# Last stage of a four-layer attention network: the wide probabilities' squares go from partition to partition in 16 DMAs a batch instead of through DRAM

## The reference

```python
h = _layernorm(x, gamma, beta)
Q = (h @ Wq).reshape(B, NQ, N_HEADS, HEAD_DIM)
K = (context @ Wk).reshape(B, NC, N_HEADS, HEAD_DIM)
V = (context @ Wv).reshape(B, NC, N_HEADS, HEAD_DIM)
attn = jnp.einsum('bihd,bjhd->bhij', Q, K)
attn = jax.nn.softmax(attn, axis=-1) * scale
vals = jnp.einsum('bhij,bjhd->bihd', attn, V).reshape(B, NQ, INNER)
out = vals @ Wo + bo
return x + out
```

## Time and profile before

| | |
|---|---|
| median of 3 runs | 1729.83 us (1729.8 to 1731.36) |
| the profiled execution's own time | 1727.86 us |
| span of that execution, first to last instruction | 1726.1 us |
| PE busy | 1638.1 us (95%) |
| DVE, ACT, POOL busy | 1310.8, 1240.9, 677.3 us |
| bytes moved by DMA | 216.51 MB |

### The profile page before, as it was taken

How to read it: one execution, slowest core, us unless ns; L and a number is a source line. 1 busy time by engine, 2 the same in 40 slices (tenths; PEclk the granted TensorE clock), 3 DMA queues, 4 the chain that set the end, 5 groups by cost and what they waited for, 6 DMA issues and landing times. The chain is left out here.

```text
span 1726.1 us, 48944 instructions
## 1 busy us (share of the span) xinstructions
PE 1638.1 (95%) x16520; PEld 1351.9 (78%) x16520; DVE 1310.8 (76%) x2408; ACT 1240.9 (72%) x3858; POOL 677.3 (39%) x946
## 2 busy tenths in 40 slices
PE   7999999999999999989899998988999999999997
PEld 6888888888888888779777777867787888787875
DVE  5777777777777777747688887656888888888885
ACT  5777777777777777623388886456888888888885
POOL 3444444454444444413222222643343434343431
PEclk9999999999999999989999999999999999999999
DMA  7776777777767767730000000014434344343441
GB/s 198 198 189 185 190 194 187 219 208 205 194 184 190 186 188 185 209 86 1 1 2 0 0 0 1 0 38 135 137 118 134 118 127 124 121 131 119 133 131 53
DMA packets 230743, 216.51 MB, mean 125 GB/s; under 512 B 19874, under 2 KB 228324, under 8 KB 230628
## 3 DMA queue, kind: packets, MB, share of 16 engines
q1 hardware_dynamic: 230628, 215.17, 45.2%
HBM read 112.34 MB, written 102.76 MB: 125 GB/s over the span
## 5 line engine op out<-in xcount | busy, mean ns | idle before, releaser
L658 ACT ACTIVATE L_probs<-L_scores,L_neg_max 128x128 f32<-128x128 f32 x512 | 182.7, 386 | 134.6 <-DVE L_neg_max L740 134.6
L854 POOL TENSOR_TENSOR L_probs<-L_probs,L_inv_sum 128x1024 f32<-128x1024 f32 x128 | 242.8, 1897 | 88.4 <-DVE L_inv_sum L760 88.4
L734 DVE TENSOR_REDUCE L_row_max<-L_scores 128x8 f32<-128x1024 f32 x128 | 156.1, 1219 | 41.5 <-PE L_scores L534 41.5
L1957 POOL TENSOR_TENSOR L2L_w_probs<-L2L_w_probs,L2L_w_inv_sum 128x1024 f32<-128x1024 f32 x64 | 121.4, 1897 | 129.7 <-DVE L2L_w_inv_sum L1783 129.5
L766 DVE STREAM_TRANSPOSE L_squares<-L_probs 128x1024 f32<-128x1024 f32 x128 | 156.6, 1223 | 0.3 <-POOL L_probs L854 0.3
L581 PE MATMUL L_ring<-L_probsT,L_v 128*64 128x128 f32 x2048 | 127.9, 277 | 9.5 <-issue 8.6
L581 PEld LDWEIGHTS L_ring<-L_probsT,L_v 128*64 128x64 f32 x2048 | 111.2, 137 | 29.9 <-issue 27.0
L534 PE MATMUL L_scores<-L_kT,L_qT 64*128 64x128 f32 x2048 | 131.8, 278 | 0.9 <-ACT L_kT L647 0.9
L534 PEld LDWEIGHTS L_scores<-L_kT,L_qT 64*128 64x128 f32 x2048 | 119.4, 188 | 12.5 <-ACT L_oT L647 8.1
L750 DVE TENSOR_REDUCE L_sums<-L_probs 128x8 f32<-128x1024 f32 x64 | 78.1, 1220 | 66.1 <-ACT L_probs L665 66.1
L1581 ACT ACTIVATE L2L_w_probs<-L2L_scores,L2L_w_neg_max 128x128 f32<-128x128 f32 x256 | 90.5, 372 | 39.3 <-DVE L2L_w_neg_max L1747 39.3
(11 more groups left out here) (220 smaller groups left out, 4617.0 us busy)
## 6 DMA issues: line engine op xcount, KB each, us to landing
L_relay<-L_squares SPq DMA_DIRECT2D x128, 512.0 KB, 3.4
L_probsT<-L_relay SPq DMA_DIRECT2D x512, 128.0 KB, 3.6
L2L_relay<-L2L_w_squares SPq DMA_DIRECT2D x64, 512.0 KB, 3.4
L2L_w_probsT<-L2L_relay SPq DMA_DIRECT2D x256, 128.0 KB, 2.9
out_x<-x SPq DMA_DIRECT2D x32, 64.0 KB, 2.7
L0a_wq<-in_L_xattn_Wq SPq DMA_DIRECT2D x2, 256.0 KB, 3.1
L0a_wk<-in_L_xattn_Wk SPq DMA_DIRECT2D x2, 256.0 KB, 3.7
L0a_wv<-in_L_xattn_Wv SPq DMA_DIRECT2D x1, 512.0 KB, 6.5
```

Of the source, the lines that this page charges most:

```text
L658: done = nc.scalar.activation(slot_probs(at, 0)[:, n, :], scores[:, 0, r, i, :], ACT.Exp, scale=layer_of(at).scale, bias=neg_max[:, n:n + ...
L734: nc.vector.tensor_reduce(row_max[:, s, :], slot(s), AX.X, ALU.max).then_inc(max_ready[s], 1)
L854: nc.gpsimd.tensor_tensor(to, to, inv_sum[:, :, s, :].unsqueeze(3) .to_broadcast([TOKENS, 2, GROUP, TOKENS]), ALU.mult).then_inc(divided, 1)
L1957: nc.gpsimd.tensor_tensor(to, to, w_inv_sum[:, :, s, :].unsqueeze(3) .to_broadcast([TOKENS, 2, GROUP, TOKENS]), ALU.mult).then_inc(w_divid ...
```

## The change

The relay in DRAM and its semaphores are gone. `w_squares` gets a second buffer. SP's `carry(at)` waits until both halves of batch `at` are turned, and issues 16 DMAs, one for each pair of blocks (i, j), each of 32 partitions x 512 elements (all 16 heads, 64 KB), from `w_squares` straight to `w_probsT`. One semaphore for each buffer counts all 16, so both halves of `w_weigh` wait for all of them, and DVE's turn waits for the landing of the batch two before in place of the relay of the batch before.

```diff
-    LANDED = 16 * SQUARES
+    LANDED = 16 * SQUARES * SQUARES
-        w_squares = sb("w_squares", [TOKENS, SQUARES, HEADS, SQUARE])
+        w_squares = sb("w_squares", [TOKENS, 2, SQUARES, HEADS, SQUARE])
-        w_relayed = [sem("w_relayed_0"), sem("w_relayed_1")]
-        w_probsT_landed = [[sem(f"w_probsT_landed_{p}{h}") for h in range(2)] for p in range(2)]
-        w_relay = [nc.dram_tensor(f"{W.name}{N.name}_relay_{h}", [TOKENS, SQUARES, SLOT_HEADS, SQUARE], FP32).ap()
-                   for h in range(2)]
+        w_probsT_landed = [sem(f"w_probsT_landed_{p}") for p in range(2)]
...
-                w_landed(pe, at, s)
+                w_landed(pe, at)
...
-                if at.n >= 1:
-                    dve.wait_ge(w_relayed[s], at.times(16, 0))
-                nc.vector.transpose(w_squares[:, :, SLOT_HEADS * s:SLOT_HEADS * (s + 1), :]
+                if at.n >= 2:
+                    w_landed(dve, at.plus(-2))
+                nc.vector.transpose(w_squares[:, at.n % 2, :, SLOT_HEADS * s:SLOT_HEADS * (s + 1), :]
...
-            def away(at, h):
-
-                sp.wait_ge(w_squares_turned, at.times(2, h + 1))
-                if at.n >= 1:
-                    w_landed(sp, at.plus(-1), h)
-                sp.dma_start(w_relay[h], w_squares[:, :, SLOT_HEADS * h:SLOT_HEADS * (h + 1), :]
-                             ).then_inc(w_relayed[h], 16)
-
-            def back(at, h):
+            def carry(at):

                 p = at.n % 2
-                sp.wait_ge(w_relayed[h], at.times(16, 16))
+                sp.wait_ge(w_squares_turned, at.times(2, 2))
                 if at.n >= 2:
-                    await_filled(sp, f"w.PV{h}", at.plus(-2))
+                    await_filled(sp, "w.PV1", at.plus(-2))
                 for j in range(SQUARES):
-                    sp.dma_start(w_probsT[SQUARE * j:SQUARE * (j + 1), p, :, SLOT_HEADS * h:SLOT_HEADS * (h + 1), :],
-                                 w_relay[h].rearrange("(i b) j h a -> j b i h a", b=SQUARE)[j]
-                                 ).then_inc(w_probsT_landed[p][h], 16)
+                    for i in range(SQUARES):
+                        sp.dma_start(w_probsT[SQUARE * j:SQUARE * (j + 1), p, i, :, :],
+                                     w_squares[SQUARE * i:SQUARE * (i + 1), p, j, :, :]
+                                     ).then_inc(w_probsT_landed[p], 16)
...
                 if here(At(t), 0):
-                    away(At(t), 1)
-                    back(At(t), 1)
-                if here(At(t), 1):
-                    away(At(t + 1), 0)
-                    back(At(t + 1), 0)
+                    carry(At(t))
```

More of the change, by code:

```diff
@@ L1339, in n_slot, with w_landed @@
             return n_probs[:, at.n % 2, s, :, :]
-        def w_landed(engine, at, h):
-            engine.wait_ge(w_probsT_landed[at.n % 2][h], at.times(LANDED // 2, LANDED - LANDED // 2 * (at.n % 2)))
+        def w_landed(engine, at):
+            engine.wait_ge(w_probsT_landed[at.n % 2], at.times(LANDED // 2, LANDED - LANDED // 2 * (at.n % 2)))
         @block.tensor
```

## The result

The changed kernel takes 1811.57 us in the median of 4 runs (1810.06 to 1818.62), beside 1729.82 us for 4 runs of the kernel before: a ratio of 1.0479, with a 95% interval from 1.045 to 1.0509. It is 82 us slower, and far outside the predicted range. The profiled execution took 1810.06 us.

The account below looks back on a forecast made before the run. PE, busy for 95% of the span, was taken as the bound, the relay as hidden. Terms 2.3 + 1.0 + 1.9 + 0.3 = +5.5 us on the profiled 1727.86 gave 1733.4, or 1735.0 for the median; range 1730 to 1750.

Parts of the forecast that it names:

- The price of an issue: On SP, 15 steps between the 16 issues, mostly 0.475 us each: 7.0 us, bounds 6.5 and 8.7.
- The landing: Time from the last of the 16 issues to its arrival in `w_probsT`: 2.4 us, bounds 2.2 and 3.1.
- the sum had 9.5: Path from the end of DVE's turn to PE's weighing: 0.03 + 7.0 + 2.4 + 0.1 us, between 8.8 and 11.9.
- So d settles at e / 2: Steady steps: if the path exceeds its cover by e, PE's late start d comes to half of e.
- ACT's slack of 0.7 us: Steady steps: the halving holds until ACT's second copy runs out of 0.7 us; from there d = e - 0.7.
- The cover of 9.78: Steady steps: 9.78 us from a batch's last turn on DVE to PE's weighing of it, leaving 0.3 us to spare.
- The ends: Pipeline filling and draining: PE waits longer before weighing batches 0 (+2.3 us), 2 (+1.0) and 30 (+1.9); batch 31: 0.
- +0.3: Row of 16 issues on SP: allowance in us for single issues that take 1.52 us instead of 0.43.
- The terms of zero: Removed relay transfers, DVE's wait for a landing two batches before, SP's wait and store issues: each worth 0.
- The overrun in every step: Rival for the steady steps: pieces cost by number, 0.57 us each, path 11.4, time 1765 (1745 if milder); chance 0.22.
- The faster case: Rival: steps where the loop turns lose their extra 1 us, up to 6 turns, giving 1727 or 1724; chance 0.06.
- the 2.2 us to spare: Kernel before: the relay's last DMA lands at 1390.5, this long before PE begins weighing at 1392.69.

Follow-up runs that it names:

- experiment 3: Changed kernel with each of the 16 DMAs carrying 4 of 16 heads (16 KB) from batch 2 on: 1803.78 us, beside 1734.32 for the kernel before.
- experiment 4: Changed kernel with its 16 DMAs reading a weight matrix in DRAM instead of the squares in SBUF: 1746.04 us, beside 1734.32 for the kernel before.
- experiment 5: Changed kernel with 16 SBUF-to-SBUF DMAs of 128 partitions x 128 elements, within their partitions: 1809.34 us, beside 1731.52 for the kernel before.
- experiment 8: Kernel before, relay kept, with only `w_squares` doubled and DVE's wait moved one batch back: 1733.10 us, beside 1731.52.
- Experiment 1: Changed kernel without the four diagonal squares' DMAs from batch 2 on, so 12 instead of 16: 1748.28 us, beside 1734.32 for the kernel before.
- experiment 7: Changed kernel with 12 DMAs from the first batch on and POOL copying the four diagonal squares: 1741.10 us, beside 1731.52 for the kernel before.

## Why the prediction was wrong

**The price of an issue failed first.** "An issue of a different shape is the nearest price" took 0.475 us from issues that read DRAM. The 15 steps took 9.4 us, not 7.0, and even the upper bound of 8.7 was too low. (Its 0.58 was no common step either: among those eight issues of the first stage one took 0.94 us, and the other steps were 0.35 to 0.64.) Experiments 3, 4 and 5 show what the rows of before could not: shape and bytes don't matter, and whether DRAM is at one end does. No row of before had both ends in SBUF; I bounded its issue by rows that differ from it in just that, as if the step could only depend on size.

**The landing was taken too long:** it was 2.0 us, where I took 2.4 and bounded it by 2.2 and 3.1. The pieces did not slow each other. With 2.4 us more for the issues and 0.4 less for the landing, the path became 11.6 us, where the sum had 9.5.

**"So d settles at e / 2" failed next,** and with it ACT's slack of 0.7 us. The overrun e is 1.8 us (11.6 - 9.78), and the step is 1.8 to 1.9 longer; the rule would have made it 1.1. I had followed ACT from its copies of the results to the turn, and left out the copy of the keys between them. That row of the kernel before, from ACT's timeline, shows that there was no slack:

```profile
1396.68 0.60 ACT L1570 ACTIVATE L2L_w_kT<-L2L_ring 128x512 f32<-128x512 f32 x1 [0.26 <-PE L2L_ring L1413]
```

ACT waits 0.26 us here for PE's projection of the keys, which stands behind the weighing in PE's order; so the turn already followed the weighing, by 7.34 us (1392.69 to 1400.03). Lateness of the weighing went round in full. The cover of 9.78 was right: 7.34 + 9.78 = 17.1, the step.

**The ends were right in kind and too small.** The waits before batch 0's and 30's weighing came as described (6.80 and 6.06 us), batch 2 has 4.06. But they rest on the path, which was 2.1 us longer, and two things were missing: the granted clock that falls around some of these waits, and single long issues in the waited rows (last section), for which I had +0.3. I had +5.2 for all ends; what lies outside batches 3 to 27 is +35.2 (22.4 + 12.8), steady overrun of those steps included, and the 3.8 by which the stage began later. Experiment 1, in which the middle fits, leaves +14.0 in all, with twelve DMAs from batch 2 on.

**The terms of zero were right.** Removing the relay wins nothing under PE's work, the second buffer nothing (experiment 8), DVE's wait for a landing never shows.

**The rivals.** The overrun in every step, which I gave 0.22, came true: the pieces cost by number and not by size. Its reason, two ends in few ports, is refuted by experiments 3 and 5, and its price of 0.57 us per piece was close to the 0.63 by chance. It reached 1765 only because it took 0.9 us of each overrun of 1.6; 27 steps x 1.6 would have made its sum 54 us, or 1784. The faster case has something in it: with the relay's traffic gone and the issues fitting, a step in which the loop turns is 17.3 to 17.8 us (experiments 1 and 4) in place of 18.0 to 18.7. That is some 0.6 us at each of five turns (I had counted six), 3 us in all, half of what was supposed, and far less than the ends cost. That it is fetched code which comes through sooner is argued, not shown.

## What to carry to other kernels

Before you put DMAs in place of others, count the issues in the row that the consumer waits for, and price one with the same memories at both ends; the bytes saved here, in a queue that was not full, were worth nothing, and each issue too many cost its full 0.63 us in every step. Then look for the circle: does the producer of the next piece wait, through any engine, for the consumer of this one? If so, there is no slack, and an overrun of one step is paid in every step. Read each row between consumer and producer for a wait, short ones too, since 0.26 us in brackets was the sign of it here.

## What the runs showed of the hardware

- **The issue on SP depends on where the two ends lie.** 0.42 us, and 0.46 from one start to the next, with DRAM as the source (experiment 4); 0.59 and 0.63 with SBUF at both ends (the changed kernel), the same for 16 KB (0.59, experiment 3), and 0.60 for 128 partitions (experiment 5). The first issue of a row is shorter in both cases: 0.31 and 0.51. The Trainium skill, "DMA: Bandwidth & Descriptors", section "Issuing engines are not separate DMA queues", calls the time it takes to initiate a DMA usually small relative to the DMA itself. In this trace one issue took 0.59 us and its landing 2.0, so it was under a third; but the issues stand in a row and the landings overlap, and the row of sixteen was 10.0 of the 11.6 us of the path.
- **A piece of 32 partitions was hardly slower than one of 128.** They landed after 2.0 and 1.9 us (experiment 5), issued 0.63 and 0.64 us apart. The rule of the Trainium skill that the prediction weighed ("SBUF — State Buffer", section "Door 1", on the ports that 32 partitions reach) set no limit at this distance.
- **An issue that follows a row of SBUF-to-SBUF issues directly is longer.** The store of a finished batch, SBUF to DRAM, takes 0.58 us right behind the 16; 0.43 before; 0.34 where it stands 0.6 us behind the row (experiments 1 and 7). Why is open.
- **Some issues take 0.8 to 1.96 us.** In the changed kernel there are 11 of them, in batches 1 to 6 and 27 to 30, and each falls on a packet that fetches instructions; the kernel before has 8, on such packets too. SP's list is unrolled. SP's timeline of the kernel after, for one such row of 16:

```profile
1271.44 11.51 SPq L1990 DMA_DIRECT2D L2L_w_probsT<-L2L_w_squares  x16
```

Before, a long issue hid in the 2.2 us to spare; in a row that is waited for it lengthens the path, up to 13.2 us for batch 5 (1271.41 to 1284.59), and the step with it. That the fetch is the cause is read from the coincidence alone; no run took the fetches away.
